# Cross-attention on one core: Wv and bv loaded ahead of the first keys, with new orders for the first and last units

## The reference, cut to what matters

```python
B, S, D, H = (4, 1024, 512, 16)        # x is (4, 2048, 512), ctx is (4, 77, 512); DK = 32
qh = _split_heads(q @ Wq.T + bq)       # q = x
kh = _split_heads(k @ Wk.T + bk)       # k = v = ctx
vh = _split_heads(v @ Wv.T + bv)
scores = jnp.einsum('bhqd,bhkd->bhqk', qh, kh) / scale
scores = jnp.where(mask == 0, jnp.asarray(-1000000000.0, scores.dtype), scores)
m = jnp.max(scores, axis=-1, keepdims=True)
e = jnp.exp(scores - m) * mask.astype(scores.dtype)
probs = e / (jnp.sum(e, axis=-1, keepdims=True) + 1e-09)
attn = jnp.einsum('bhqk,bhkd->bhqd', probs, vh)
out = attn @ Wo.T + bo
x = out + residual                     # residual = q
return (x - mu) / jnp.sqrt(var + 1e-05) * ln_g + ln_b
```

## Time and profile before

| | us |
|---|---|
| median of 3 runs (lowest to highest) | 602.46 (601.54 to 602.71) |
| the profiled execution, its own time | 604.55 |
| its span, first to last instruction | 602.8 |
| PE busy in the span | 568.3 (94%) |
| DVE, ACT, POOL busy | 528.6, 501.3, 436.9 |
| mean granted TensorE clock | 0.979 of full speed |

### The profile page before, as it was taken

The page is one execution under the profiler, slowest core; times in us unless marked ns, Lnnn a source line. Parts: engine busy times, 40 slices in busy tenths (PEclk is TensorE's granted clock), DMA queues, the critical chain, the costliest instruction groups (busy, mean ns, idle before and its releaser), DMA issues.

```text
span 602.8 us, 15264 instructions
## 1 busy us (share of the span) xinstructions
PE 568.3 (94%) x5460; PEld 461.3 (77%) x5460; DVE 528.6 (88%) x803; ACT 501.3 (83%) x2284; POOL 436.9 (72%) x401
## 2 busy tenths in 40 slices
PE   3978888999999999999999999999999999998894
PEld 3866666787878788787878788887878788786673
DVE  4586998899999989898999989898999989899776
ACT  4339979889989999899979998899979997899421
POOL 3223677368695886799777985799777986797797
PEclk9989888999999999999999999999999999999798
DMA  8558220220325201730145212520425212302142
GB/s 306 157 181 252 108 81 11 72 82 3 128 71 216 72 18 58 250 124 21 47 149 196 90 54 75 200 87 3 151 76 197 82 53 102 110 19 88 73 140 104
DMA packets 36198, 64.91 MB, mean 108 GB/s; under 512 B 12443, under 2 KB 14491, under 8 KB 34075
## 3 DMA queue, kind: packets, MB, share of 16 engines
q1 hardware_dynamic: 35979, 63.94, 31.2%
q10 hardware_dynamic: 144, 0.00, 0.0%
HBM read 44.15 MB, written 19.46 MB: 106 GB/s over the span
## 4 chain that ended last, share of the span: by engine, by line
PE 84%; DVE 8%; DMA 3%; SPq 2%; issue 2%; ACT 0%; DVEq 0%; POOL 0%
PE qo_bank L534 28%; PE qo_bank L430 26%; PE s_bank L430 17%; PE av_bank L520 10%; DVE E L854 1%; DVE WoT_lo L811 1%; PE av_bank L445 1%; PE s_bank L534 1%; DMA TP<-in_WvT 1%; DMA K_scratch<-TP 1%; DVE TP L883 1%; SPq L318 1%; DVE bn L906 1%; PE av_bank L430 1%; DMA E<-in_ctxT 1%
## 5 line engine op out<-in xcount | busy, mean ns | idle before, releaser
L678 ACT ACTIVATE E<-E,neg_max 128x77 f32<-128x77 f32 x1024 | 352.4, 354 | 30.2 <-DVE neg_max L862 30.2
L678 ACT ACTIVATION_READ_ACCUMULATOR E<-E,neg_max 128x1 f32 x1024 | 198.6, 194 | 0.0
L1165 POOL TENSOR_TENSOR E<-E,inv_sum 128x1232 f32<-128x1232 f32 x64 | 145.3, 2278 | 40.7 <-DVE inv_sum L869 40.7
L854 DVE TENSOR_TENSOR E<-s_bank,mask_bias 128x616 f32<-128x616 f32 x128 | 101.2, 791 | 23.2 <-PE s_bank L430 21.6
L430 PE MATMUL s_bank<-Kd,QT_hi 128*128 128x308 f32 x512 | 112.8, 307 | 0.0
L862 DVE TENSOR_REDUCE neg_max<-E 128x8 f32<-128x624 f32 x128 | 99.4, 783 | 0.4
L883 DVE STREAM_TRANSPOSE TP<-E 128x1280 f32<-128x1280 f32 x64 | 95.0, 1494 | 1.0 <-issue 0.6
L430 PE MATMUL s_bank<-Kd,QT_lo 128*128 128x308 f32 x256 | 81.9, 320 | 12.7 <-DVE E L854 12.7
L430 PEld LDWEIGHTS s_bank<-Kd,QT_hi 128*128 128x128 f32 x512 | 85.5, 191 | 4.4
L1183 POOL TENSOR_TENSOR Y<-Y,b_row 128x512 f32<-128x512 f32 x62 | 79.5, 1304 | 3.6 <-ACT Y L695 3.5
L1156 POOL TENSOR_TENSOR Y<-Y,bo_row 128x1024 f32<-128x1024 f32 x32 | 77.2, 2428 | 0.0
...
## 6 DMA issues: line engine op xcount, KB each, us to landing
...
```

The lines of the kernel that those rows point to most:

```text
L678: last = cp(e, e, ACT.Exp, bias=neg_max[:, t, h:h + 1], accum_out=rowsum[:, t, h:h + 1])
L854: tt(E[:, t, :, 0:SK].rearrange("p (g j) k -> p g j k", g=2), s_bank[:, :, 0:GK].rearrange("p g (j k) -> p g j k", j=HG), mask_bias[:, row ...
L1165: nc.gpsimd.tensor_tensor(out=e, in0=e, in1=inv.unsqueeze(2).broadcast_to((P, 2 * HH, SK)), op=ALU.mult).then_inc(probs_ready, 1)
```

## The change

SP issues Wv's four quarters and bv directly behind the last of Wq, ahead of `load_K(0)` and so ahead of its wait for the first keys. `later_loads()` keeps `zero_V`, Wo, bo, g and b behind `load_K(0)`. No step is added or removed on any engine, and none is changed in size; the orders of steps are arranged anew at both edges, and a few neighbours are swapped in the pattern.

```diff
@@ -366,10 +372,11 @@
             load_half("k", WkT, 1)
             load_half("q", WqT, 1)
 
+            for c in range(C):
+                load_w("v", WvT, c)
+            load_row(bv_loaded, bv_row[:, :], bv)
+
             def later_loads():
-                for c in range(C):
-                    load_w("v", WvT, c)
-                load_row(bv_loaded, bv_row[:, :], bv)
                 zero_V()
                 for c in range(C):
                     load_w("o", WoT, c)
...
                 if s == -3:
-                    K(0), K(1), Q(0, 0), Q(0, 1), Q(0, 2), Q(0, 3), S(0, 0)
+                    K(0), K(1), Q(0, 0), Q(0, 1), Q(0, 2), Q(0, 3), K(2), S(0, 0), K(3), S(0, 1), V(0)
+                    S(0, 2), V(1), S(0, 3), Q(1, 0)
...
                 if s == -3:
-                    XT_hi_1(0), XT_hi_1(1)
+                    XT_hi_1(0), XT_hi_1(1), split_hi_q(2)
                 elif s == -2:
-                    split_hi_q(2)
-                elif s == -1:
-                    split_hi_q(3)
+                    split_hi("v", 0), split_hi("v", 1)
                 elif s == 0:
-                    split_hi("v", 0), split_hi("v", 1), split_hi("v", 2), split_hi("v", 3), pads()
+                    split_hi("v", 2), split_hi("v", 3), split_hi("o", 0)
```

More of the change, by code:

```diff
@@ L950, in _ @@
-                    split_lo("q", 1)
+                    split_lo("v", 0), split_lo("v", 1), split_lo("v", 2), split_lo("v", 3), Q_lo(0, 2)
                 elif s == -1:
-                    XT_lo_first(1, 0), XT_lo_first(1, 1), Q_lo(0, 0), K_lo(0), K_lo(1), split_lo("k", 2)
-                    split_lo("k", 3), Q_lo(0, 1), masks(), split_lo("v", 0), split_lo("v", 1)
-                    split_lo("v", 2)
+                    bias(0, 0), bias(0, 1), row_max(0, 0), row_max(0, 1), split_lo("q", 2), split_lo("q", 3)
@@ L955, in _ @@
+                    bias(0, 2), row_max(0, 2)
                 elif s == 0:
-                    Q_lo(0, 2), Q_lo(0, 3), split_lo("v", 3), bias(0, 0), bias(0, 1), split_lo("o", 0)
-                    row_max(0, 0), split_lo("q", 2), split_lo("q", 3), V_add(0), bias(0, 2), K_lo(2)
-                    K_lo(3), row_max(0, 1), row_max(0, 2)
+                    K_lo(2), K_lo(3), bias(0, 3), row_max(0, 3), Q_lo(0, 3), V_add(0), V_add(1), bias(0, 4)
+                    row_max(0, 4), inverse(0, 0), inverse(0, 1), V_add(2), bias(0, 5), row_max(0, 5)
@@ L959, in _ @@
+                    bias(0, 6), turn(0, 0), Q_lo(1, 0)
                 elif s == 1:
[L960 to L963 removed]
+                    row_max(0, 6), bias(0, 7), row_max(0, 7), Q_lo(1, 1), inverse(0, 2), bias(1, 0)
@@ L964, in _ @@
+                    row_max(1, 0), turn(0, 1), inverse(0, 3), bias(1, 1), turn(0, 2), bias(1, 2)
                 elif s == 2:
[L965 to L968 removed]
@@ L983, in _ @@
                     row_max(3, 3), bias(3, 4), turn(3, 0), row_max(3, 4), bias(3, 5), Q_lo(4, 0)
-                    AT_lo_(2, 0), AT_lo_(2, 1), AT_lo_(2, 2), row_max(3, 5), Q_lo(4, 1), inverse(3, 1)
-                    residual(1, 0), stats(1, 0), AT_lo_(2, 3), aggregate(1, 0), bias(3, 6), center(1, 0)
+                    AT_lo_(2, 0), AT_lo_(2, 1), AT_lo_(2, 2), AT_lo_(2, 3), row_max(3, 5), Q_lo(4, 1)
+                    residual(1, 0), inverse(3, 1), stats(1, 0), aggregate(1, 0), bias(3, 6), center(1, 0)
@@ L1031, in _ @@
                     row_max(13, 2), bias(13, 3), residual(10, 2), residual(10, 3), stats(10, 2)
-                    stats(10, 3), bias(13, 4), aggregate(10, 2), inverse(13, 0), aggregate(10, 3)
-                    center(10, 2), row_max(13, 3), center(10, 3), bias(13, 5), turn(13, 0), Q_lo(14, 0)
-                    row_max(13, 4), row_max(13, 5), AT_lo_(12, 0), AT_lo_(12, 1), AT_lo_(12, 2), Q_lo(14, 1)
-                    residual(11, 0), stats(11, 0), bias(13, 6), inverse(13, 1), aggregate(11, 0)
@@ L1194, in _ @@
                 elif s == 1:
-                    split_hi("o", 0), split_hi("o", 1), split_hi("o", 2), add_eps(0, 0), add_eps(0, 1)
-                    normalise(0, 0), normalise(0, 1), split_hi("o", 3), add_eps(0, 2)
+                    pads(), split_hi_q(3), add_eps(0, 0), add_eps(0, 1), normalise(0, 0), add_eps(0, 2)
+                    normalise(0, 1), normalise(0, 2), add_eps(0, 3)
                 elif s == 2:
-                    normalise(0, 2), add_eps(0, 3)
+                    normalise(0, 3), split_hi("o", 1), split_hi("o", 2), split_hi("o", 3), XT_lo(2, 0)
@@ L1208, in _ @@
-                    add_eps(3, 1), add_beta(0, 0), add_beta(0, 1), normalise(3, 1), add_beta(0, 2)
-                    add_beta(0, 3)
+                    normalise(2, 1), add_eps(2, 3), normalise(2, 2), normalise(2, 3), inv_std(0, 0)
+                    inv_std(0, 1), XT_lo(4, 0), XT_lo(4, 1), add_eps(3, 0), normalise(3, 0), XT_lo(5, 0)
+                    XT_lo(5, 1), add_eps(3, 1), inv_std(0, 2), inv_std(0, 3), add_beta(0, 0), add_beta(0, 1)
+                    normalise(3, 1)
                 elif s == 5:
-                    add_eps(3, 2), normalise(3, 2), add_eps(3, 3), normalise(3, 3), add_bo(2, 0)
```

338 lines of the change are left out of this document (179 added, 159 removed).

## The result

The changed kernel takes 596.72 us (median of 4 runs, 596.23 to 597.65) against 602.00 us (4 runs, 601.36 to 602.71): a ratio of 0.9903, with a 95% interval of 0.9884 to 0.9923 (the two medians alone give 0.9912, which lies in it). The forecast was 595.8 us, with a range of 592.6 to 599.0. The profiled execution took 597.65 us, with a span of 595.9 us, 6.9 under the 602.8 of before.

A forecast was written before the change was run, and what follows sets the result against it. PE was taken as the bound, busy 408.92 of 409.50 us from 105 to 514.5 us, so early gains carry to the end. 7.4 - 0.7 = 6.7 us off the 602.46 median gave 595.8 us, range 592.6 to 599.0.

The forecast's parts named there:

- Part one: At the start, early Wv removes the 3.44 us wait ahead of S(0,1) and slow clock behind it: 5.1 us by S(0,2).
- The clock term of 1.64 us: From S(0,1) to S(0,2): V(0) no longer runs at the lower clock once the wait ahead goes; gain 1.64 us.
- rival D: At the first bias: it waits for `pads`, and `pads` for Wo's first quarter; 2 us slower, 604.8 us; chance 0.04.
- Part two: Units 0 and 1: Q(1,1) moved and keys saved earlier give 1.2 and 0.5 us; turn(0,3) 7.4 us earlier, about 61.9.
- The term for Q(1,1): Q(1,1) between S(0,6) and S(0,7) leaves one wait of about 0.9 us instead of two; gain 1.2 us.
- Part three: Ahead of S(1,5): four low parts of Wo in one row, slowed by POOL's XT_lo, give back 0.7 of 7.4 us.
- The shared rate: Alternative for Wo's low parts: DVE and POOL share bandwidth, 2.29 us each, S(1,5) at 76.7, gain 5.0 us.
- From there to 105 us I take the difference at 0: From S(1,5) to 105 us: orders nearly the same, difference 0; longer slow stretch put at 0 to 1.2 us, taken as 0.
- Part four: From Q(15,0) on: the 3.33 us wait stays and moves along; `store(13,0)` ahead of `load_rows(14)` costs 0, at most 0.8 us.
- rival C: At the end: DVE or ACT, not PE, sets the pace and the gain is returned; 601.5 to 602.5 us; chance 0.04.
- A: Wo's low parts all blocked, or 1 to 2 us lost in units 2 to 4 and 13; gain 3.2 to 5.3; chance 0.15.
- B: Wo's splits are freer: XT_lo finished or DVE reaches them later; gain 8.2 to 11, time 591.5 to 594.3; chance 0.12.

The follow-up runs named there:

- the loads alone: The kernel before with Wv and bv issued behind Wq, ahead of the first keys, all engines' orders as before: 598.28 us, ratio 0.9938.
- the changed kernel again: The changed kernel unedited, timed once more beside the kernel before: 597.35 us over 6 runs, ratio 0.9921.

## Why the prediction was right

**Part one, the loads: right.** V(0) ran at full clock, and S(0,2) came 5.9 us earlier with 5.1 foretold. Of the 5.9, 0.7 stand ahead of Q(0,0), where the prediction has no term, so that much of the agreement is luck; counted from Q(0,0) it is 5.3 against the first trace of before and 5.0 against the mean of three, and the loads alone give the same. (K(2) stands ahead of S(0,0), as the prediction has it, and K(3) behind it; the text on the change puts both between S(0,0) and S(0,1).) Wv was converted from 19.3 on (20.5 foretold), and the keys' store was issued at 39.85 (40.5 foretold). The clock term of 1.64 us is of the kind that can be counted on: from S(0,1) to S(0,2) it takes 5.28, 5.29 and 5.29 us in three traces of before, and 3.64, 3.63 and 3.64 in three of the changed kernel. What the prediction did not see is that the new order of DVE alone would also have removed most of the wait, by letting SP's wait for the first keys end 5 us earlier. It named that as a fact against rival D and not as a second cause.

**Part two: right.** turn(0,3) started at 61.42, foretold 61.9; counted from Q(0,0) that is 7.2 us earlier, foretold 7.4. The term for Q(1,1), 1.2 us, measures 1.2 at AV(0,0) and 1.4 at S(1,5). S(1,2) and S(1,3) wait 0.90 and 0.97 us, where 0.85 and 1.3 were foretold, so that term of 0.5 came out as 0.8.

**Part three: right in mechanism and nearly in size.** 7.36 us for 7.5 (7.6 by its own sum), S(1,5) at 74.4 for 75.0, a wait of 3.54 for 3.9. One by one the four took 1.17, 2.89, 2.84 and 0.70 us, where 1.28, 2.87, 2.87 and 0.68 were foretold. Each of the first three ends 0.55 us behind the end of an XT_lo that had begun ahead of it (67.41, 70.22 and 72.98 behind 66.87, 69.67 and 72.43), and the two XT_lo that begin behind the start of a low part take 2.8 us instead of 2.4: the two engines take turns, an instruction at a time. The other side is shown too: without XT_lo beside them the four take 2.51 us. The Trainium skill, SBUF — State Buffer, section "Who interferes with whom", has it as an exclusive lock. The shared rate that was weighed against it would have put S(1,5) at 76.7, and 74.4 is measured. The step that was mis-sized is the clock behind this wait. "It already cost the clock before" was true of the one trace and of one in three: from S(1,5) to S(2,1) before takes 14.48, 13.71 and 13.71 us, the changed kernel 14.47, 14.46 and 14.37. So a term put at 0, inside its range of 0 to 1.2, measures 0.8 us against two of three traces and 0.5 against their mean.

**"From there to 105 us I take the difference at 0":** nearly right, a loss of 0.4 us in the mean of three traces each, which is the clock term just named. The 1.2 us won there in the first pair of traces (8.6 at AV(1,0) for 7.4 at S(1,5)) is the half clock at 100.7 us, which comes and goes in both kernels.

**Part four, the end: the wait as foretold, one loss unseen.** The wait of 3.33 us ahead of OUT(13,2) stands in every kernel, whatever the gain ahead of it, so rival C is out: the gain was carried. The sign of being wrong that the text named, a new wait between 100 and 507 us, did not come. But at 506.94 the gap that stood in before as 0.69 us ("issue") is 1.19, and in the profiled execution the half clock behind it cost another 1.5. PE's order there is the same, and the prediction, which looked at waits for other engines only, had no term for it: 0.5 us, and 2 when the clock falls behind it, which it did in one of nine traces. The price of 0 for `store(13,0)` ahead of `load_rows(14)` was right: in the profiled execution POOL waited 0.98 us for that load and began add_bo(14,0) at 568.27, 6.0 us earlier than before, and residual(14,0) followed at 570.80, 6.1 earlier, as OUT(13,2) did.

**The sum.** 6.7 us were foretold by S(1,5). 7.1 were won over three traces each, of which 0.7 stand ahead of Q(0,0) and 6.4 belong to the steps that the prediction adds up. 5.3 are left in the medians. The terms left out (0.5 to 0.8 of clock behind S(1,5), 0.5 of gap, 0.2 in the middle units) account for the difference to within the clock of single executions. The time was 0.9 us over the forecast, and that is closer than the working deserves: the gain fell short by 1.4 us, and the kernel before, measured beside the changed one, had a median of 602.00 and not the 602.46 that the forecast starts from. There was also a warning: the one trace on which all was built was 2.1 us over its kernel's median, and the prediction subtracted a gain measured in it from the median. Its half-clock stretches at 82 and 100 us are missing in one or both of the other two traces, and its wait of 3.44 us ahead of S(0,1) is 3.21 and 2.95 there.

**The rivals.** A expected small losses in units 2 to 4 and 13 and a gain of 3.2 to 5.3. Its losses are there, but smaller than its 1 to 2 us: 0.5 at AV(13) and 0.2 in between. The gain of 5.3 stands on the border between A and the forecast, and by time 596.72 lies just inside the forecast's 597.2, while the changed kernel again, at 597.35, lies just outside (both are within the stated range of 592.6 to 599.0). B was the wrong way. C is out, as said. D's chain exists and cost 1.1 us once Wv was put back. In the changed kernel itself it has slack: Wo's first quarter is there at 25.3, `pads` done by 26.6, `bias(0,0)` begins at 28.5.
